# A graph-network layer whose edge-aggregation batches are moved together ahead of each unit

## What is computed

```python
for t in range(T):                      # 3 edge types, weights of their own
    emask = (edge_type == t)
    h = x
    for i in range(STEPS):              # 3 steps
        m = h @ W[i]
        msg = m[src] * emask[:, None]
        agg = segment_sum(msg, dst)     # sum of the messages that reach a node
        r = sigmoid(agg @ wih_r + h @ whh_r + b)
        z = sigmoid(agg @ wih_z + h @ whh_z + b)
        n = tanh(agg @ wih_n + b + r * (h @ whh_n + b))
        h = (1 - z) * n + z * h
    h_msg = h_msg + h
```

## Time and profile before

| | |
|---|---|
| Time, median of 3 runs | 3880.06 us |
| The profiled execution | 3884.5 us, its span 3882.8 us |
| Mean granted TensorE clock | 0.841 |
| PE busy | 2948.0 us (76%) |
| DVE busy | 1994.2 us (51%) |
| POOL busy | 1700.8 us (44%) |
| ACT busy | 836.0 us (22%) |
| PE matmuls of the batches, L1003 | x4716, 486.3 us busy, 210.1 us idle before them |
| One-hots, L1079 | x393, 319.2 us |
| Adds, L1072 | x393, 217.7 us |

### The profile page before, as it was taken

One profiled execution on the slowest core, in us unless ns is written; L12 is line 12 of the kernel. 1 busy time (PEld: TensorE's weight loads), 2 busy tenths in 40 slices (PEclk: granted clock), 3 DMA queues, 4 the chain that ended last, 5 costly groups with the idle time before them and its releaser, 6 DMA issues. The chain is left out here.

```text
span 3882.8 us, 61285 instructions
## 1 busy us (share of the span) xinstructions
PE 2948.0 (76%) x19834; PEld 1946.5 (50%) x19834; DVE 1994.2 (51%) x3409; ACT 836.0 (22%) x1454; POOL 1700.8 (44%) x1616
## 2 busy tenths in 40 slices
PE   1466666888895999994899997599999150599990
PEld 1244543555553565652565664355555040488880
DVE  4599997777424565654465554455554641000002
ACT  1233333444300111121111112011111030232220
POOL 0144443444205777742777770677773004000005
PEclk6677777888666999997899999699999655799995
DMA  1200000000035444533355441444442322411103
GB/s 39 75 0 0 0 0 1 0 0 0 3 124 184 143 151 144 153 116 109 117 153 157 150 148 49 149 125 124 122 127 74 73 78 90 152 60 63 60 19 102
DMA packets 182014, 333.29 MB, mean 86 GB/s; under 512 B 27487, under 2 KB 134908, under 8 KB 181213
## 3 DMA queue, kind: packets, MB, share of 16 engines
q0 software_dynamic: 61968, 167.46, 14.7%
q1 hardware_dynamic: 119884, 163.82, 12.8%
HBM read 245.01 MB, written 86.17 MB: 85 GB/s over the span
## 5 line engine op out<-in xcount | busy, mean ns | idle before, releaser
L1155 POOL DMA_INDIRECT g_ring<-h_rows,idx x786 | 795.8, 1012 | 454.5 <-issue 222.7
L1003 PE MATMUL g_pagg<-g_onehot,g_ring 128*128 128x192 f16 x4716 | 486.3, 257 | 210.1 <-DMA g_ring<-h_rows,idx 149.7
L1003 PEld LDWEIGHTS g_pagg<-g_onehot,g_ring 128*128 128x128 f16 x4716 | 420.0, 102 | 383.8 <-issue 216.1
L1155 POOL DMA_INDIRECT g_ring<-xn_rows,idx x393 | 396.2, 1008 | 293.4 <-PEq L1198 174.0
L1072 DVE TENSOR_TENSOR g_agg<-g_agg,g_pagg 128x384 f32 x393 | 217.7, 554 | 417.8 <-PE g_pagg L1003 390.9
L1079 DVE SCALAR_TENSOR_TENSOR g_onehot<-iota_keys,g_shift,keys 128x576 f16<-128x576 f16 x393 | 319.2, 813 | 0.6 <-DVE g_at L1221 0.6
L1628 DVE TENSOR_TENSOR f_ys<-f_p,f_b 128x256 f32<-128x256 f32 x58 | 24.6, 425 | 533.9 <-PE f_p L1603 533.9
L715 POOL TENSOR_TENSOR mq_Fl<-mq_F,mq_Fh 128x448 f16<-128x448 f32 x168 | 191.4, 1166 | 233.6 <-ACT mq_Fh L700 229.9
L1649 POOL DMA_INDIRECT fc_y<-slots_out,slot_of x56 | 52.0, 929 | 509.7 <-PEq L1643 492.9
L502 PE MATMUL mk_pm<-mk_v,mk_Fh 112*128 112x33 bf16 x3360 | 159.8, 189 | 149.4 <-issue 149.4
L502 PEld LDWEIGHTS mk_pm<-mk_v,mk_Fh 112*128 112x128 f16 x3360 | 157.4, 104 | 160.2 <-issue 160.0
(11 more groups left out here) (277 smaller groups left out, 5146.3 us busy)
## 6 DMA issues: line engine op xcount, KB each, us to landing
h_cols<-g_hn SPq DMA_DIRECT2D x42, 448.0 KB
h_rows<-g_rowb SPq DMA_DIRECT2D x42, 448.0 KB
g_hT<-h_cols SPq DMA_DIRECT2D x42, 448.0 KB, 7.4
f_w<-in_L_ffn_W SPq DMA_DIRECT2D x16, 1024.0 KB
g_ring<-h_rows,idx POOLq DMA_INDIRECT x786, 2.8
g_hT<-xn_cols SPq DMA_DIRECT2D x21, 448.0 KB, 7.2
slots_in<-fg_none SPq DMA_DIRECT2D x64, 128.0 KB, 1.7
ft_x<-slots_in SPq DMA_DIRECT2D x8, 1024.0 KB
```

What stands on the lines that cost most here:

```text
L1003: mm = e.matmul(pg[:, k * TYPES:(k + 1) * TYPES, :].rearrange("p t d -> p (t d)"), ring[:, b % SLABS, c, o:o + P], onehot[:, b % 3, c, :], ...
L1155: e.indirect_dma_start(ring[:, b % SLABS, c, :], None, tables[s], bass.IndirectOffsetOnAxis(ap=idx[:, q:q + 1], axis=0)).then_inc(landed[b ...
```

## The change

One expression in `batches_before` is changed: the position is rounded down to a multiple of four.

```diff
 def batches_before(pos):
 
-    return min(NB, LEAD - (-pos * (NB - LEAD) // SPREAD)) if pos >= 0 else 0
+    return min(NB, LEAD - (-(pos - pos % 4) * (NB - LEAD) // SPREAD)) if pos >= 0 else 0
```

## The result

| | before | after |
|---|---|---|
| Time, median | 3880.99 us (4 runs) | 3941.24 us (4 runs, 3936.91 to 3943.38) |
| Ratio after / before | | 1.0154, 95% interval 1.0137 to 1.0172 |
| Span of the profiled execution | 3882.8 us | 3939.9 us |

The change makes the kernel 60 us slower. The forecast was 3906 us, 26 us slower, with a range up to 3932 us; the direction was right, the size was not.

A forecast was written before the change was run, and what follows sets the result against it. PE and POOL's gathers were taken to run at almost one pace. Handovers +68, gather waits -37, clock -15 and base tile +9.5 gave +26 us: 3910 us profiled, 3906 us forecast, range 3870 to 3932.

The forecast's parts named there:

- What bounds the kernel: In the streams, PE at 13.0 us a unit and POOL's gathers at 13.16 run side by side; PE waits the difference.
- The handover: Inside a row, the third one-hot stands behind an add on DVE: batch at T + 2.63, 0.65 us lost per row.
- The fourth batch's 0.2 us: A row's fourth batch waits for DVE's pace of 1.19 us against 0.99: 0.20 us more, in 12 rows a step.
- What later batches take away: In the streams, PE's gather waits fall from 43.1 to 6 us, -37 us; less time at lower clock, -15 us.
- 68 - 37 - 15: Over three steps: +68 us net for gaps inside rows, -37 us of gather waits, -15 us of lower clock.
- The base tile: Last step: one-hots queue behind DVE's wait for the `g_base` load; PE waits 1.9 us in five groups, +9.5 us.
- Nothing is gained or lost on ACT and SP: On ACT and SP, instructions keep their order, so no time was added or taken away.
- The nine slabs: POOL never waits for a free slab: a batch finished up to 9 us later is inside nine slabs, 35 us.
- DVE comes late as a whole: Rival: a late reset gate delays a whole row; longest base load in five groups adds 43 us, about 3949 us; chance 0.10.
- the gathers set the end: Rival, last batch of each stream: PE keeps inside POOL's pace, saving 6.8 us a step, 3860 us; chance 0.11.
- The clock did not fall: Rival: the clock falls at 105 gaps, 1.4 us each, +147 us on the forecast, 4053 us; chance 0.03.

The follow-up runs named there:

- b_late: Kernel before with the early load of `g_base` and the last batch at the first block of unit 36 (SPREAD 144, was 140): 3846.4 us, ratio 0.9916.
- a_base: Changed kernel with SP issuing the load of `g_base` right behind the transposes, ahead of the store and next `g_hT` load: 3896.8 us, ratio 1.0038.
- a_copy: Changed kernel with ACT's copies of the transposed rows moved ahead of their unit's tanh, in the last step alone: 3912.7 us, ratio 1.0082.
- a_hots_base: Changed kernel with a row's one-hots ahead of its adds and the early load of `g_base`: 3885.0 us, ratio 1.0016.
- a_hots: Changed kernel with six one-hot buffers instead of three, a row's one-hots written before its adds, PE waiting for adds itself: 3924.9 us, ratio 1.0103.
- pairs_base: Changed kernel with the position rounded down to a multiple of two, not four, and the early load of `g_base`: 3892.5 us, ratio 1.0033.
- pairs: Changed kernel with the position rounded down to a multiple of two instead of four: 3896.5 us, ratio 1.0037.

## Why the prediction was wrong, step by step

**What bounds the kernel: right.** PE and the gathers at almost one pace. b_late shows it from the other side: moving the batches later up to one unit, which leaves PE's work and the end of the gathers as they are, wins 34 us.

**The handover: right.** 2.63 us worked out, 2.63 us measured in the median, at nearly all of the 35 rows a step. The fourth batch's 0.2 us show in no wait, but in the length: the third and fourth batch mostly span 2.36 us together where two that are ready take 2.14.

**What later batches take away: right, a little more.** Waits for gathers fell from 43.1 to 3.4 us (6 forecast) and the clock in steps 0 and 1 rose to 1.00. Together with the handover this gave +8.9 and +4.2 us where about 10 and 7 were forecast. By the runs, the change without the base tile costs 16 us (a_base), and the forecast's 68 - 37 - 15 is 16 us too; since its parts are each off by some us, that this comes out so exactly is in part luck.

**The base tile: the step that failed.** The forecast took the load's landing from the kernel before, 12.1 us behind the transposes' end, and only moved the one-hots behind it. It even noted that the candidate would end up to 4.4 us behind T, the end of the update block, and tanh some 1.4 us later, and yet said "Nothing is gained or lost on ACT and SP: their instructions keep their order". The order was kept and the times were not. ACT's copies of the rows stand behind tanh, so the store, the next `g_hT` and the load of `g_base` came 4.2 us later (8.9 instead of 4.7 us), and the load took 8.9 us from issue to use instead of 8.2. The wait was 6.6 to 7.7 us five times, 35 us in all, with the lower clock behind each. Forecast +9.5 us; measured 44 us (changed kernel against a_base). An estimate from the rows gives the same: 35 us of waits, five rows of batches with a mean span of 5.6 us and not 3.1, less five handovers of 0.65 us that these rows don't have, make 44 us. a_copy shows the link: ACT's order alone gives 28.5 us back and leaves waits of 2.4 us, near the forecast's 1.9. The other 16 us (3912.7 - 3896.8) are the wait that the forecast did see. It put it at 9.5 us; the waits alone are 12 us, and the clock behind the longer ones was no term of the sum.

**The nine slabs: wrong, without effect.** The forecast had POOL never waiting, as a batch that ends 9 us later is still well inside them. In the stream of step 2 POOL waited for PE 21 times, 38.8 us in all and 8.7 at most, since PE itself had fallen behind. PE waited for no gather there, so this cost nothing.

**The rivals.** "DVE comes late as a whole" named this place and the price per microsecond, with 3949 us, but gave the load's own length as its cause; it had a chance of 0.10. That the gathers set the end is excluded for the change itself by PE's 3.4 us of waits for them, and fits a_hots_base, where they are 50 us. The clock did not fall at the 0.65 us gaps: 1.00 in the windows of steps 0 and 1, with 34 gaps in each. The Trainium skill's page "TensorE: Matmul & The Clock Gate" (section "A second HAM failure mode: psum-queue depth-cycling") tells of short idles between groups of matmuls, whose length it doesn't give, under which the clock oscillates; here gaps of 0.65 us had no such effect, while the waits of 4.87 us and 6.60 us were each followed by a stretch at 1.2 GHz.

## What to carry to other kernels

When an instruction that waits is moved ahead of others on one engine, follow each result that becomes late through the other engines' queues, until it lands in a transfer: unchanged order on an engine is not unchanged time, and a copy that stands behind an activation delays the store, and with it the loads behind it on the same queue. A transfer that waits for a free buffer is best issued right behind what frees it, ahead of other loads on its queue: this gave 44 us in the changed kernel, and nothing in the kernel before, where DVE's wait for the load delayed nothing that PE needed. Where two engines run at one pace, moving work later in its stream gains only what is left to do behind the last transfer; here one unit less was worth more than any order of the batches.

## What the runs showed of the hardware

POOL's gathers, which in the kernel before never waited for PE longer than 0.3 us, differ in length with what DVE does: 0.95 us beside an idle DVE, 1.25 us in the mean beside one-hots that stand in rows (a_hots, step 0), and 1008, 1031, 1038 and 1041 ns in the mean of step 0 for the kernels before, pairs_base, pairs and a_hots. The Trainium skill, "SBUF — State Buffer", section "SBUF: two separate sides", says that VectorE and GpSimd share a port pair by an exclusive lock, and that while VectorE runs an op in a 2-port perf mode GpSimd can't write the descriptors of its transfers. The traces agree in direction; whether the one-hot is such an op, and whether the lock is the cause, no run here shows.

A load takes about twice as long from issue to landing when three others stand right ahead of it on SP's queue: `g_base` lands after 8.2 us in the median behind the three loads of `g_hT` (kernel before), and after 3.9 us ahead of them (a_base).
